# The last three head groups of a decoder layer, run by halves of the batches

## The reference

```python
x = x + attn(layernorm(x))                  # 128 heads of 4 + 64 columns, latent size 64
x = x + xattn(layernorm(x), ctx, positions) # 32 query heads, 8 key heads of 16, rope
x = x + ffn(layernorm(x))                   # base matmul + 2 of 8 LoRA experts
# attn: scores = (q_c @ k_c^T + q_r @ k_r^T) / sqrt(68), q_r = x @ Wq_rope (512 x 8192)
#       out = softmax(scores) @ v_c, then out @ Wo
```

## Time and profile before

| | |
|---|---|
| median of 3 runs | 868.87 us (867.58 to 870.23) |
| the profiled execution | 867.85 us |
| its span | 865.9 us |
| PE busy | 803.9 us, 93% |
| DVE busy | 647.9 us, 75% |
| ACT busy | 568.5 us, 66% |
| POOL busy | 582.8 us, 67% |
| loop over head groups ends | 607.2 us |
| `turn(0)` of the second part | 671.8 us |

### The profile page before, as it was taken

How to read it: one execution, slowest core, us unless ns; L and a number is a source line. 1 busy time by engine, 2 the same in 40 slices (tenths; PEclk the granted TensorE clock), 3 DMA queues, 4 the chain that set the end, 5 groups by cost and what they waited for, 6 DMA issues and landing times.

```text
span 865.9 us, 17867 instructions
## 1 busy us (share of the span) xinstructions
PE 803.9 (93%) x5624; PEld 395.2 (46%) x5624; DVE 647.9 (75%) x1209; ACT 568.5 (66%) x1045; POOL 582.8 (67%) x492
## 2 busy tenths in 40 slices
PE   4999999999999999999999999999848688999986
PEld 3464444444454444444444444444313344555433
DVE  7866777767677888777888767788787567888754
ACT  4757777777777777777777777777530465555641
POOL 7747888888788878888888878885543223333210
PEclk9999999999999999999999999999978799999999
DMA  8344455434334332434333433432130000000001
GB/s 334 110 166 146 92 156 169 139 85 112 101 90 105 85 108 78 107 97 123 85 82 91 113 104 89 109 89 56 29 88 0 1 1 3 15 13 15 13 13 37
DMA packets 51227, 74.69 MB, mean 86 GB/s; under 512 B 9968, under 2 KB 33520, under 8 KB 50672
## 3 DMA queue, kind: packets, MB, share of 16 engines
q1 hardware_dynamic: 51184, 74.18, 30.7%
HBM read 38.16 MB, written 18.87 MB: 66 GB/s over the span
## 4 chain that ended last, share of the span: by engine, by line
PE 84%; DVE 8%; ACT 2%; issue 2%; DMA 1%; SPq 1%; POOL 0%; DVEq 0%; ACTq 0%
PE PS L1200 39%; PE PS L1152 8%; PE PS L1236 7%; PE PS L1266 6%; PE PS L1268 6%; PE PS L1283 5%; PE PS L1411 2%; PE PS L1325 1%; PE PS L1418 1%; PE PS L1380 1%; PE PS L1397 1%; PE PS L1426 1%; PE PS L1456 1%; DVE xm L1027 1%; PE PS L1244 1%
## 5 line engine op out<-in xcount | busy, mean ns | idle before, releaser
L492 POOL TENSOR_TENSOR Pl<-PR,Ph 128x512 f16<-128x512 f32 x254 | 285.8, 1157 | 24.7 <-ACT Ph L668 24.7
L661 ACT ACTIVATE PR<-PS 128x512 f32<-128x512 f32 x256 | 152.6, 597 | 135.0 <-PE PS L1268 128.5
L795 DVE TENSOR_REDUCE mneg<-PS 128x4 f32<-128x512 f32 x256 | 174.6, 684 | 38.2 <-PE PS L1236 34.7
L1200 PE MATMUL PS<-XTh,Wh 128*128 128x512 f16 x512 | 194.5, 380 | 0.0
L1200 PE MATMUL PS<-XTh,Wl 128*128 128x512 f16 x512 | 193.7, 378 | 0.0
L1200 PE MATMUL PS<-XTl,Wh 128*128 128x512 f16 x512 | 193.5, 378 | 0.0
L783 DVE SCALAR_TENSOR_TENSOR QS<-PS,QC 64x512 f16<-64x512 f32 x256 | 175.5, 686 | 18.0 <-ACT QC L593 10.9
L593 ACT ACTIVATE QC<-PS 64x512 f16<-64x512 f32 x256 | 150.7, 589 | 10.6 <-PE PS L1200 4.3
L668 ACT ACTIVATE Ph<-PR 128x512 f16<-128x512 f32 x256 | 139.3, 617 | 0.0
L474 POOL TENSOR_TENSOR Wh<-Wraw,wscale 128x1024 f16<-128x1024 f32 x32 | 60.6, 1893 | 70.8 <-PE PS L1200 67.5
L1236 PEld LDWEIGHTS PS<-KC,QC 112*128 112x128 f16 x1024 | 78.8, 97 | 62.2 <-issue 2.7
(11 more groups left out here) (213 smaller groups left out, 1163.4 us busy)
## 6 DMA issues: line engine op xcount, KB each, us to landing
Wraw<-in_wqr SPq DMA_DIRECT2D x32, 512.0 KB, 4.6
QS<-QC SPq DMA_DIRECT2D x64, 256.0 KB, 3.2
head_outputs<-OS SPq DMA_DIRECT2D x256, 40.0 KB
q_content_parts<-stg SPq DMA_DIRECT2D x12, 256.0 KB, 2.8
k_content_parts<-stg SPq DMA_DIRECT2D x12, 256.0 KB, 3.1
QC<-q_content_parts SPq DMA_DIRECT2D x128, 24.0 KB
KC<-k_content_parts SPq DMA_DIRECT2D x32, 96.0 KB
xs<-in_x SPq DMA_DIRECT2D x8, 256.0 KB, 4.5
```

The costliest lines, as they stand in the source:

```text
L492: nc.gpsimd.tensor_tensor(Pl[:, b], PR[:, b % 4], Ph[:, b], ALU.subtract).then_inc(s_pl, 1)
L661: nc.scalar.activation(PR[:, b % 4, :], PS[:, bB[b % 2], :], ACT.Exp, scale=ATT_SCALE).then_inc(s_e, 1)
L795: nc.vector.tensor_reduce(mneg[:, par, b // 4, :, b % 4], PS[:, bA[b % 2], :].rearrange("p (j k) -> p j k", j=GH), AX.X, ALU.max, negate=T ...
L1200: last = mm(PS[:, bQ[c % 2], :], wt[:, par, k, p * P:(p + 1) * P], xt[:, k, sl], start=(k == 0 and n == 0), stop=(k == KT - 1 and n == 2))
```

## The change

Halves are counted through as jobs 0 to 63. Jobs 0 to 57 are as before. The last six are reordered: groups 29, 30, 31 for batches 0 to 3, then groups 31, 30, 29 for batches 4 to 7. The split weights of group 29 are overwritten in between, so they are stored to DRAM and read back. Content rows come for each half by itself, with a second pair of key buffers (KC2). The last quarter of the head outputs is gathered in two halves of the batches, the first after job 60. `turn(0)` waits for four x1 and not for eight. Further edits: the weight splits of groups 30 and 31 are shared between ACT and POOL; DVE takes one of the four rests of two jobs; `angles` moves into halves 22 to 25; three of the four weight splits, `k_rope(1)` and the last two batches' sums move into units 1 to 4 of the second part; the memsets of kst and qst go.

```diff
+LG = 3
+G0 = NG - LG
+LATE = NH - 2 * LG
+TURN = LATE + LG
+def job(h):
+    if h < LATE:
+        g, t, k = h // 2, h % 2, h // 2 % 2
+    else:
+        g = G0 + h - LATE if h < TURN else NG - 1 - (h - TURN)
+        t, k = h // TURN, (0, 2, 1, 3)[h % 4]
+    return Job(g, t, h, h // 2, h // 2 % 2, h % 2, k, g % 2)
+BY_DVE = range(LATE - 3, TURN - 4)
...
 # SP
+            def late_contents(j):
+                sp.wait_ge(s_b, 4 * (j.n - 3))
+                sl = slice(j.t * HALF, (j.t + 1) * HALF)
+                for i in range(GH):
+                    r = CROW + CR * i
+                    sp.dma_start(QC[r:r + CR, j.p, j.s, i, :], YD[j.g * GH + i, :, sl]).then_inc(s_yl[j.n % 4], 16)
+                if j.k >= 2:
+                    sp.wait_ge(s_kc, 4)
+                sp.dma_start(kc(j.k)[CROW:MROW, sl], XD[j.g * GH:(j.g + 1) * GH, :, sl].rearrange("h r k -> (h r) k")
+                             ).then_inc(s_yl[j.n % 4], 16)
...
+            def late_half(h):
+                maxima(job(h - 2))
+                if h == NH - 2:
+                    sp.wait_ge(s_q, 2 * h)
+                    sp.wait_ge(s_wst, 16)
+                    sp.dma_start(W16[:, G0 % 2], WD[0]).then_inc(s_wr, 16)
+                q_again(job(h - 1))
+                if h + 1 < NH:
+                    late_contents(job(h + 1))
+                outputs(job(h - 4))
+                if h == LATE:
+                    sp.wait_ge(s_ws, G0 + 1)
+                    w_in(NG - 1, G0 % 2)
+                    sp.dma_start(WD[0], W16[:, G0 % 2]).then_inc(s_wst, 16)
...
+            def half_quarter(t, j):
+                for s in range(2):
+                    sp.wait_ge(s_od[s], 64 * (NG if t else (TURN + 1 - s) // 2))
+                sp.wait_ge(s_un, B * (KT - 2) + B // 2 * (t + 1))
+                gather(KT - 1, j, t * B // 2, (t + 1) * B // 2, s_ue if t else s_ud[KT - 1])
...
+            late_contents(job(LATE))
+            for h in range(LATE, NH):
+                late_half(h)
+            maxima(job(NH - 2))
+            outputs(job(NH - 4))
+            q_again(job(NH - 1))
+            maxima(job(NH - 1))
             for j in range(GH):
-                gather(KT - 1, j)
+                half_quarter(0, j)
+            outputs(job(NH - 3))
+            outputs(job(NH - 2))
+            sp.wait_ge(s_b, 4 * NH)
             sp.dma_start(lb_sb[:], lb).then_inc(s_ffn, 16)
             sp.dma_start(bias[:], bb.to_broadcast([P, DM])).then_inc(s_ffn, 16)
+            outputs(job(NH - 1))
+            for j in range(GH):
+                half_quarter(1, j)
...
 # GpSimd, ahead of its loop
+            nc.gpsimd.memset(KC2[96:P], MS).then_inc(s_zero, 1)
+            for i in range(2):
+                nc.gpsimd.tensor_copy(KC2[0:RD, i, :], KS[0:RD, :]).then_inc(s_kc, 1)
 # GpSimd, in halves 58 and 59, in two column halves p
+                    nc.gpsimd.tensor_tensor(w, w, wscale[:].to_broadcast([P, KT, P]), ALU.mult).then_inc(s_wd2, 1)
+                    nc.gpsimd.tensor_tensor(Wl[:, par, :, p * P:(p + 1) * P], w, Wh[:, par, :, p * P:(p + 1) * P], ALU.subtract
+                                            ).then_inc(s_wp, 1)
...
 # ScalarE, in halves 58 and 59, ahead of p_high and exps
+            def late_high(g):
+                par = g % 2
+                act.wait_ge(s_w[par], 16 * (g // 2 + 1))
+                act.wait_ge(s_q, 2 * (LATE + g - 1 - G0))
+                if g == NG - 1:
+                    act.wait_ge(s_wst, 16)
+                nc.scalar.activation(Wh[:, par], Wraw[:, par], ACT.Copy, scale=WS).then_inc(s_wa, 1)
...
+            q_high(job(NH - 1), 1)
+            p_high(job(NH - 3))
             act.wait_ge(s_wx, 16)
+            act.wait_ge(s_q, 2 * NH)
+            split_high(0)
+            for n in (NH - 2, NH - 1):
+                for b in range(4):
+                    exps(job(n), b)
+                p_high(job(n))
...
+                if u in (1, 2, 3):
+                    if u == 1:
+                        act.wait_ge(s_ffn, 48)
+                        act.wait_ge(s_pv, NH)
+                    split_high(u)
...
 # VectorE; part 0 holds posf, ang and three turns, part 2 three turns, parts 1 and 3 the other five each
+            def half(g, par, t):
+                J = lambda d: ago(g, par, t, d)
+                h = 2 * g + t if isinstance(g, int) else None
+                if J(1) and later(J(1).n, 2):
+                    q_low(J(1), 1)
+                if J(4):
+                    o_out(J(4))
+                if h == 2:
+                    max_out(job(0))
+                if h is not None and 22 <= h < 26:
+                    angles(h - 22)
                 for b in range(4):
+                    row_max(J(1), b)
+                    if b == 1 and h is not None:
+                        for piece in shares(h):
+                            inverse_sums(*piece)
+                    if b == 2 and h is not None and h - 3 in BY_DVE:
+                        p_low(J(3))
+                q_low(J(0), 0)
+                if h is not None:
+                    for piece in shares(h):
+                        apply_sums(*piece)
+                max_out(J(1))
...
+            o_out(job(NH - 4))
+            q_low(job(NH - 1), 1)
+            for b in range(4):
+                row_max(job(NH - 1), b)
+            normalise(KT - 2, 6)
+            max_out(job(NH - 1))
+            normalise(KT - 2, 7)
+            split_low(0)
+            o_out(job(NH - 3))
+            o_out(job(NH - 2))
+            normalise(KT - 1, 0)
+            normalise(KT - 1, 1)
             x1(0)
-            dve.wait_ge(s_x1, 1)
             for u in range(FIRST, LAST):
...
                 if u == FIRST:
+                    rope_factors()
+                if u == FIRST + 1:
+                    x1(1)
+                    k_rope(0)
+                if u == FIRST + 2:
                     normalise(KT - 1, 2)
+                    o_out(job(NH - 1))
+                if u == FIRST + 3:
                     normalise(KT - 1, 3)
                     x1(2)
+                if u == FIRST + 4:
+                    x1(3)
+                if u == -1:
+                    for v in range(B // 2, EARLY):
+                        normalise(KT - 1, v)
+                    for v in range(B // 2, EARLY):
                         x1(v)
+                if u in (1, 2, 3):
+                    split_low(u)
+                if u in (1, 3):
+                    normalise(KT - 1, 6 + u // 2)
+                if u == 2:
+                    k_rope(1)
+                if u in O1_AT:
+                    x1(O1_AT[u])
...
 # TensorE, behind its loop
+            for i in range(4):
+                rough_scores(job(NH - 1), i)
+                if i < KT - 1:
+                    output(0, i)
+            for i in range(4):
+                scores(job(NH - 2), i)
+                if i < KT - 1:
+                    output(1, i)
+                if i == 0:
+                    max_turn(job(NH - 1))
+            weigh(job(NH - 3))
+            for T in range(KT - 1):
+                output(2, T)
+            for i in range(4):
+                scores(job(NH - 1), i)
+                if i < KT - 1:
+                    output(3, i)
+            weigh(job(NH - 2))
+            output(0, KT - 1)
+            pe.wait_ge(s_e, 4 * NH)
+            for T in range(KT - 1):
+                output(4, T)
+            weigh(job(NH - 1))
+            output(1, KT - 1)
...
                 if u == -2:
-                    pe.wait_ge(s_x1, B)
+                    pe.wait_ge(s_x1, B // 2)
+                    pe.wait_ge(s_kx, 2)
```

More of the change, by code:

```diff
@@ L1 @@
 import math
+from collections import namedtuple
 from contextlib import ExitStack
@@ L293, in seated, with looped, spelled @@
             return filled[max(filled.index((kind, n)) - 4, 0)]
-        def looped(eng, step, first, last):
+        def looped(eng, half, first, last):
             with eng.Fori(0, (last - first + 1) // 2) as i:
-                step(2 * i + first, 1)
-                step(2 * i + first + 1, 0)
-        def spelled(step, first, last):
+                for g, par in ((2 * i + first, 1), (2 * i + first + 1, 0)):
+                    for t in range(2):
+                        half(g, par, t)
+        def spelled(half, first, last):
             for g in range(first, last + 1):
-                step(g, g % 2)
-        def g_is(g, n):
-            return isinstance(g, int) and g == n
+                for t in range(2):
+                    half(g, g % 2, t)
         def reached(g, first, behind=0):
@@ L401, in _ @@
             store(2)
-            q_again(0, 0, 0)
-            spelled(step, 1, 1)
+            q_again(job(0))
+            spelled(half, 1, 1)
             store(3)
-            spelled(step, 2, 2)
+            spelled(half, 2, 2)
             sp.wait_ge(s_yx[3], 16 * 6)
@@ new lines, in half @@
+            def half(g, par, t):
+                J = lambda d: ago(g, par, t, d)
```

(43 more changed lines are left out.)

713 lines of the change are left out of this document (367 added, 346 removed).

## The result

The changed kernel takes 893.76 us (892.8 to 894.5), the kernel before 868.84 us beside it: a ratio of 1.0286, 95% interval 1.0266 to 1.0306. The forecast was 879.5, within 861 to 889: slower as said, but by 25 us and not by 11. The profiled execution took 894.5 us with a span of 892.8, 26.9 more than the span before.

What follows compares the result with a forecast made beforehand. PE was taken to bound the loop, then a chain of waits behind it. Angles 14.9, clock 5, store 5.5, late maxima and rests 0.5, tail -14.5: +11.4 on 867.85, forecast 879.5; own range 866 to 889, with the faster rival from 861.

Steps and rivals of the forecast that it cites:

- the angles' mechanism and their waits: Halves 22 to 25: POOL holds DVE's 18 angle instructions ahead of the row maxima, stalling PE by 14.9 us in sum.
- the clock: After stalls of PE in the loop: mostly 1.2 GHz for 4 us, about 1.6 us each, three of five taken, 5.
- the store: Half 59: ACT's `late_high(31)` waits until group 29's weights are stored, and PE for ACT: 5.5 us (3 to 7.5).
- about their reserve: Half 59: the maxima come 1.5 to 2 us late, about their reserve; with DVE's extra rests put at 0.5.
- Then units 1 to 4 pay back: Behind the loop: DVE gets 11.5 us more work in units 1 to 4; unit 5's maxima at about +84, not +99.4.
- -14.5: Behind the loop up to unit 5's maxima: gain 15.5, of which 1 is given up for clock (-10 to -20).
- PE's last output of batch 7: Units 1 to 4: this output, at +79.1, waits for the sum that DVE made in unit 3.
- The tail gives it back: Rival, behind the loop: second half gather or DVE's work in units 1 to 4 takes 5 to 8 us more; 886; chance 0.15.
- The tail wins: Rival: DVE's angles get in beside POOL (2.7) and the tail gives 18; about 857, or 866.5 with half the hold; chance 0.2.
- The store is hidden: Rival: half 59 costs nothing and the rest stands; 874; chance 0.2.
- It doesn't do what it says: Rival: the first half gather waits for all stores and `turn(0)` stays where it was; 893 or more; chance 0.02.
- the lowest corner: Lowest end of the forecast's range: angles 12.3, clock 0, store 3, tail -20; said to be already no change or faster.

Runs made afterwards that it cites:

- e11: Changed kernel with only PE's outputs of batches 6 and 7 put behind the weighing and DVE's two products made earlier: 884.51 us, 1.0209 of the kernel before.
- the run with all repairs: Changed kernel with angles in POOL's gaps, store in half 58, early splits, outputs behind the weighing, `k_rope(1)` at u = 6: 859.48 us, 0.9899 of the kernel before.

## Why the prediction was right and wrong

**Right: the angles' mechanism and their waits.** Held by POOL one for one, 14.0 us of waits for 14.9. Two runs with POOL idle and busy and one in the kernel before show the cause.

**Mis-sized: the clock.** The prediction gave a stall 1.6 us of clock and took three of five stalls, 5 in all. The price was right for three of the angles' stalls (1.7 each); the first, of 5.2 us, cost 2.5, and all four brought the clock down. So the four cost 8.1 instead of some 4, and the two short waits of half 59 cost nothing.

**Mis-sized, the other way: the store.** 5.5 reckoned, with about 1 of clock beside it, and 3.8 measured. That ACT waits for the store and PE for ACT is seen, and ACT's wait goes with an earlier store; but 1.8 of PE's 3.3 us of waits are for the late row of maxima, whose lateness the prediction had put into "about their reserve". With the store moved, 2.1 or 1.0 us stay, according to SP's order.

With both, the loop's end was right to 1.2 us, since the misses of 22.1 - 18.9 and 3.8 - 6.5 cancelled for the most part; 0.8 was there from the start. That is luck as much as reckoning.

**Wrong: the step "Then units 1 to 4 pay back", and with it -14.5.** Unit 5's maxima came at +98.0, forecast near +84. Of these 14 us, 5.4 were lost by `x_scores(0)` (+58.4 for +53), 4.2 of them ahead of `turn(0)`; no run singled that piece out. The other 8.6 lie between it and unit 5's maxima: 31 us were forecast there, 39.6 measured, 24.3 before. The prediction walked through DVE's order alone (+64.4, +72.2, +78.2) and let PE in only at the end, with "PE's last output of batch 7". (Its list of additions to DVE sums to 11.3 us, not 11.5, which changes nothing.) But PE's stream has `output(6, 3)` at u = 2 ahead of the rough scores of unit 4. DVE's lateness is handed to PE, and PE hands it back to DVE's next maxima, once more at u = 4. The maxima of unit 2 were due soon after +64.4 by DVE's order, and came at +73.4. PE's waits at these outputs sum to 8.5 us (2.72, 1.86 for `xs`, 3.95), and for the clock, at 0.71 to 0.83 over 60 us, 1 us had been given up. The run of the changed kernel in which only the order differs, of PE's outputs and DVE's two products (e11), gets 9.2 us back, 6.7 by the ratios.

**The rivals.** "The tail gives it back" had the right side and 0.15; it put 5 to 8 us on the gather or on DVE's load. The gather was innocent, and the size was 13.2. "The tail wins" needed DVE to get in beside POOL, and it doesn't. "The store is hidden" falls with ACT's 4.59 us. "It doesn't do what it says" named 893, the time that came, but not its cause: `turn(0)` did move ahead, by 22.4 us. Of the range, the lowest corner (12.3 + 0 + 3 + 0.5 - 20) lies 4.2 below the kernel before, at 864 and not at the 866 at which the forecast's own range begins.

What stays open is the bound of about +87 at unit 5 when the circle is open. It is 12.4 us better than before, while unit 0's maxima come 18.2 earlier (+57.2). Of the 5.8 between, the clock at 0.59 in 660 to 680 of the run with all repairs is a part that no experiment here took apart. Nor did any touch PE's wait of 4.4 us at `output(4, 3)` in step -1, which is of the same kind as those at batches 6 and 7 and stands in the changed kernel and in every run with the repaired tail.

## What to carry to other kernels

Price a move into a busy loop by what the neighbour engine does at that very moment: 18 small instructions cost 22 us beside POOL's rests, 16 beside its weight splits and nothing in its gaps, and a wait of the bound engine can cost its clock as well. When work is spread over later stages, walk through the streams of both engines together, unit by unit: an in-order instruction that waits for the late piece holds all that the other engine needs next. Then the repair is a matter of order: here moved instructions and DMAs alone turned a change that lost 2.9% into one that gains 1%.

## What the runs showed of the hardware that was not expected

- Each of four stalls, of 5.2, 3.4, 2.1 and 3.3 us, with PE busy before and after, was followed by 3 to 5 us at 1.2 GHz (0.50) and then by 2.4 GHz again (1.00). The three shorter ones cost 1.7 us of clock each, whatever their length, the longest 2.5. Two waits of 1.8 and 1.0 us in half 59 left the clock at 1.00.
- DVE's smallest instruction is held as the others are: the cast of 8 columns took 0.15 us with POOL idle, 0.52 and 0.89 beside it. In the tail, `agl` took 0.72 us in the run with all repairs and 1.78 in the changed kernel, where a multiplication of 1.77 us on POOL began 0.56 us ahead of it.
